# Four edits to a one-core graph network kernel: row sums by small SBUF-to-SBUF transfers, natural unit order, a new load order, and another root in the last tail

## The chip, the cores and the metric

The kernel runs on one core of one Trainium2 chip. The time is the device time in microseconds of one execution of the whole program; the number for a kernel is the median of its runs. TensorE (PE in the profile) multiplies matrices into PSUM, VectorE (DVE), ScalarE (ACT) and GpSimd (POOL) work elementwise, and SyncE (SP) issues the transfers (DMAs). Engines run on their own and wait for each other by semaphores.

## The reference

There are 64 graphs of 128 nodes with 128 features. Each passes four layers, with a layer norm over features behind each, added to its input (residual):

```
L0:  hi = x W1[:H], hj = x W1[H:]
     h[i,j] = relu(hi[i] + hj[j] + b1)           # 128 x 128 pairs, 128 features
     y[i,j] = h[i,j] W2 + b2 ;  y = layernorm(y, gamma, beta)
     out[i] = sum_j adj[i,j] y[i,j]
L1:  relu((D^-1/2 adj D^-1/2 x) W^T + b)
L2:  relu(((1+eps) x + adj^T x) W1 + b1) W2 + b2, masked
L3:  three times  h = relu(layernorm(adj^T (h W) + b + h))
```

L0 is nearly all of the work: 16,384 pairs a graph. The kernel folds the layer norm of a pair into one coefficient, c[i,j] = adj[i,j] / deviation[i,j]. Then out[i] is the sum over j of c[i,j] h[i,j], multiplied once by the centred W2 times gamma, plus the row sum of c times the centred b2 times gamma, plus adj times beta. Those **row sums of c** are what the first edit is about.

## The kernel before

**Units, duos, slots.** A unit is one node i with all 128 partners j: h of a unit is a 128x128 tile, made by one instruction relu(vT + uT[:, i]). Eight units are a duo, worked on in one of 16 slots of a graph. In each slot TensorE makes the duo's products (L417, two matmuls of 512 columns, each run as two passes, so two rows of the profile each), ScalarE squares them (L566), and in every second slot TensorE sums the squares over features (L429). Three engines share the h units: VectorE (`vector_units`: 4, 0 or 1), GpSimd (`pool_units`: 3 in the slots listed in ROOTLESS, otherwise 2) and ScalarE the rest. GpSimd makes fewer where it also has the two-step root of a norm (L912 adds eps, L915 raises to -0.5).

**Order of the work.** Everything is written out by hand, with no scheduler. Each engine runs the same loop over iterations and 16 slots; a slot is cut into nine fine places. Work of a graph lags: h in slot 4 on, products in slot 5 on, squares in slot 6, the weighted sums of h by c (L685, on VectorE) 19 slots later. The later layers of a graph ("the tail") run beside the pairs of two later graphs, at places given in the table `AT` as (slot, fine place), counted from two iterations after the graph began.

**The path of a coefficient.** ScalarE takes the root of half a graph's variances (L573). SyncE straightens the rows to one unit-half per partition (L324). VectorE takes the reciprocal (L693) and multiplies by adj (L701); the same instruction leaves the sum of each partition's 64 columns in `c_row_sum`. One partition holds half a unit's row, so a unit's row sum is the sum over two partitions. SyncE stores c to DRAM (L335) and broadcasts it to all partitions in five transfers (L347, L349). On the way SP waits in program order for each step.

**The row sums before.** At the end of slot 8 VectorE copies `c_row_sum` (L869). At place (1, 4) TensorE adds the pairs of partitions and puts them in unit order by two matmuls with a 0/1 matrix `row_pick` (L450), which the profile shows as four rows of 128x1. VectorE copies the result (L740) and uses it for `x_base` (L744). The matrix is needed because units are numbered in the order in which the transfers lay them out (`unit_of`); adj is loaded for this order in eight transfers a graph (L288).

**Start and end.** All seven first weights carry one semaphore, and TensorE waits for all of them and for VectorE's centring of W2 and b2 (L808 to L821). The last graph's tail runs with nothing beside it; its seven norms use GpSimd's root like all others.

Of the kernel before, what the change touches and what calls it, by code (L numbers as in the profile page):

```python
# [8 lines left out]
ALU = mybir.AluOpType  # L9
# [3 lines left out]
P = 128  # L13
# [90 lines left out]
def build(nc, x, adj, nodemask, l0_W1, l0_b1, l0_W2, l0_b2, l0_gamma, l0_beta, l1_W, l1_b,  # L104
# [4 lines left out]
    with ExitStack() as ctx:  # L109
# [6 lines left out]
        def sem(name):  # L116
# [42 lines left out]
        row_pick, rows_sum = sb("row_pick", [P, 2, P]), sb("rows_sum", [P, 2])  # L159
# [55 lines left out]
        row_pick_set, rows_kept, c_summed, c_sum_set = (  # L215
            sem("row_pick_set"), sem("rows_kept"), sem("c_summed"), sem("c_sum_set"))
# [60 lines left out]
        def _(sp):  # L277
# [6 lines left out]
            def load_adj_c_rows(a):  # L284
                rows = a.rearrange("(h q p n) (l j) -> h p q (n l) j", h=2, q=4, p=CHUNKS, l=2)
# [42 lines left out]
            def store_coefficients(g, half):  # L328

                wait_apart(sp, c_made, 2 * g + half + 1)  # L330
                for p in range(CHUNKS):
# [4 lines left out]
                             ).then_inc(c_stored[half], 16)  # L336

# [51 lines left out]
        def _(pe):  # L389
# [44 lines left out]
            def later_layers(g, b, lo, hi):  # L434
# [18 lines left out]
                if due("l0_mm"):  # L453
                    wait(pe, c_sum_set, g + 1)
# [32 lines left out]
            def later_set_up():  # L487
# [482 lines left out]
```

## Time and profile before

| | |
|---|---|
| median of 3 runs | 2756.13 us (2755.44 to 2756.31) |
| the profiled execution | 2755.1 us, its span 2753.5 us |
| PE busy | 2690.3 us, 98% |
| DVE busy | 2619.0 us, 95% |
| ACT busy | 2567.7 us, 93% |
| POOL busy | 2487.8 us, 90% |
| granted TensorE clock | 9 tenths or more in every slice but the last, 5 tenths there |
| DMA | 208 GB/s on average |
| one steady graph | 41.85 us, 62 times nearly alike |

A busy share counts any time in which an instruction is in flight. Matmuls overlap, so a busy TensorE is not TensorE at its peak. PEld is the weight load of a matmul; it can go while the matmul ahead of it runs. In a row of the timeline the bracket at the end gives how long the engine had been idle and what it waited for; "xN" means N like instructions merged, from the start of the first to the end of the last.

### The profile page before, as it was taken

What the parts mean: (1) busy time and instruction counts of PE and PEld (TensorE: products, weight loads), DVE (VectorE), ACT (ScalarE), POOL (GpSimd) and SP (SyncE); (2) the same over time, 40 slices, a digit from 0 to 9 for tenths busy, and PEclk for the clock granted to TensorE, in tenths of its full rate; (3) what the DMA queues carried; (4) which work ended last, traced back from release to release, by engine and by line L of the source; (5) the groups of instructions that cost most, each with busy time, mean ns of one, the idle gap of its engine ahead of it and who ended that gap; (6) DMA issues with size and microseconds to landing.
All of it is one profiled execution on the core that took longest, in us unless ns stands there. A gap on an engine that the chain in (4) does not pass through costs nothing.

```text
span 2753.5 us, 60836 instructions
## 1 busy us (share of the span) xinstructions
PE 2690.3 (98%) x10882; PEld 1147.3 (42%) x10882; DVE 2619.0 (95%) x20102; ACT 2567.7 (93%) x6903; POOL 2487.8 (90%) x3498
## 2 busy tenths in 40 slices
PE   8999999999999999999999999999999999999993
PEld 2344444444444444444444444444444444444442
DVE  4999999999999999999999999999999999999997
ACT  7999999999999999999999999999999999999991
POOL 3899999999999999999999999999999999999992
PEclk9999999999999999999999999999999999999995
DMA  3655655655555555556556555555655565565562
GB/s 108 237 196 209 231 206 196 231 219 194 215 231 201 202 226 219 197 215 231 199 200 232 214 194 221 227 199 203 230 213 197 214 236 196 202 234 210 195 228 95
DMA packets 188668, 571.72 MB, mean 208 GB/s; under 512 B 70656, under 2 KB 106368, under 8 KB 139136
## 3 DMA queue, kind: packets, MB, share of 16 engines
q1 hardware_dynamic: 188288, 567.83, 54.5%
q14 instruction: 285, 2.33, 0.3%
q8 instruction: 95, 1.56, 0.2%
HBM read 555.17 MB, written 8.39 MB: 205 GB/s over the span
## 4 chain that ended last, share of the span: by engine, by line
PE 67%; ACT 18%; DVE 8%; issue 6%; POOL 1%; DMA 0%; SPq 0%; ACTq 0%; DVEq 0%; POOLq 0%
PE y_ps L417 47%; PE ss_ps L429 13%; ACT h L556 11%; DVE h L685 5%; ACT sq L566 4%; ACT dev_rows L573 2%; PE prod_bank L479 1%; PE prod_bank L483 1%; PE prod_bank L450 1%; ACT hid L595 1%; PE prod_bank L456 1%; PE prod_bank L457 1%; PE uv_ps L402 1%; PE uv_ps L403 1%; POOL h L924 1%
## 5 line engine op out<-in xcount | busy, mean ns | idle before, releaser
L924 POOL TENSOR_SCALAR h<-vT,uT 128x128 f32<-128x128 f32 x2520 | 2056.7, 831 | 23.7 <-ACT vT L546 23.3
L417 PE MATMUL y_ps<-h,w2c 128*128 128x512 f32 x4096 | 2016.4, 609 | 11.4 <-DVE h L669 1.6
L685 DVE CUSTOM_DVE_ANT_0 h<-h,cb 128x128 f32<-128x128 f32 x8192 | 1983.9, 289 | 10.0 <-DVE gT_keep L749 0.5
L556 ACT ACTIVATE h<-uv_ps,uT 128x128 f32<-128x128 f32 x4848 | 1409.2, 433 | 0.0
L566 ACT ACTIVATE sq<-y_ps,b2c_col 128x1024 f32<-128x1024 f32 x1024 | 1182.5, 1155 | 112.3 <-PE y_ps L417 112.1
L417 PEld LDWEIGHTS y_ps<-h,w2c 128*128 128x128 f32 x4096 | 682.2, 190 | 903.6 <-issue 723.7
L685 DVE DVE_READ_ACCUMULATOR2_ANT gT<- 128x1 f32 x8192 | 636.8, 78 | 0.1
L429 PE MATMUL ss_ps<-sq,sel 128*32 128x512 f32 x4096 | 545.5, 605 | 0.9 <-ACT sq L566 0.9
L915 POOL TENSOR_TENSOR rs<-var_eps,minus_half 128x1 f32<-128x1 f32 x448 | 302.7, 676 | 35.1
L669 DVE TENSOR_SCALAR h<-vT,uT 128x128 f32<-128x128 f32 x757 | 200.9, 294 | 4.7 <-ACT mask_all L611 2.6
L912 POOL TENSOR_TENSOR var_eps<-mv,eps_col 128x1 f32<-128x1 f32 x448 | 96.1, 215 | 117.9 <-DVE mv L712 115.0
L429 PEld LDWEIGHTS ss_ps<-sq,sel 128*32 128x32 f32 x4096 | 80.6, 108 | 225.5 <-ACT sq L566 105.0
L709 DVE BATCH_NORM_STATS2 stats<-z 128x6 f32<-128x128 f32 x448 | 127.4, 284 | 0.3
L483 PEld LDWEIGHTS prod_bank<-l3w,aggT 128*128 128x128 f32 x384 | 73.6, 194 | 93.0 <-issue 58.6
L693 DVE RECIPROCAL invs<-devs 128x64 f32<-128x64 f32 x128 | 70.1, 548 | 38.6 <-DMA devs<-dev_rows 35.6
L718 DVE TENSOR_SCALAR x<-z,mv,rs 128x128 f32<-128x128 f32 x256 | 96.7, 378 | 6.2 <-POOL rs L915 4.8
L907 POOL TENSOR_TENSOR dis_raw<-degree_floor,minus_half 128x1 f32<-128x1 f32 x64 | 35.1, 548 | 65.3 <-DVE degree_floor L733 65.3
L599 ACT ACTIVATE aggT<-prod_bank 128x128 f32<-128x128 f32 x192 | 66.3, 345 | 25.3 <-PE prod_bank L479 21.7
L604 ACT ACTIVATE h<-z_aff 128x128 f32<-128x128 f32 x192 | 70.4, 367 | 17.5 <-DVE z_aff L792 17.5
L792 DVE SCALAR_TENSOR_TENSOR z_aff<-z_aff,rs,l3beta 128x128 f32<-128x128 f32 x192 | 81.9, 427 | 4.6 <-POOL rs L915 2.9
L573 ACT ACTIVATE dev_rows<-ss_ps 128x512 f32<-128x512 f32 x128 | 79.8, 624 | 1.2 <-PE ss_ps L429 1.2
L712 DVE BATCH_NORM_AGGREGATE mv<-stats 128x2 f32<-128x6 f32 x448 | 77.8, 174 | 2.6
(100 smaller groups left out, 1489.8 us busy)
## 6 DMA issues: line engine op xcount, KB each, us to landing
cb<-c_scratch SPq DMA_DIRECT2D x384, 1024.0 KB, 9.3
cb<-c_scratch SPq DMA_DIRECT2D x256, 512.0 KB, 4.8
adj_c<-in_adj_dram SPq DMA_DIRECT2D x512, 8.0 KB
devs<-dev_rows SPq DMA_DIRECT2D x512, 8.0 KB
x_in<-in_x_dram SPq DMA_DIRECT2D x64, 64.0 KB, 10.8
c_scratch<-c SPq DMA_DIRECT2D x128, 32.0 KB, 1.5
adj_in<-in_adj_dram SPq DMA_DIRECT2D x64, 64.0 KB, 4.4
x_res<-in_x_dram SPq DMA_DIRECT2D x64, 64.0 KB, 5.4
```

Source lines behind the costliest of these rows:

```text
L417: op = pe.matmul(y_ps[:, t % 2, c0:c0 + COLS], w2c[:], h[:, (SLOTS * g + t) % H_RING, c0:c0 + COLS], start=True, stop=True)
L429: mm = pe.matmul(ss_ps[32 * q:32 * q + 32, :], sel[:, ROWS - 1 - p:ROWS - 1 - p + 32], sq[:, (t + q // 2) % SQ_RING, c0:c0 + COLS], start= ...
L483: pe.matmul(out, aggT[:, b, :], l3w[:, i, :], start=True, stop=False)
L556: op = act.activation(h[:, (SLOTS * g + t) % H_RING, n * P:(n + 1) * P], v, ACT.Relu, bias=uT[:, b, i:i + 1])
L566: act.activation(sq[:, t % SQ_RING, :], y_ps[:, t % 2, :], ACT.Square, bias=b2c_col[:], scale=float(P) ** -0.5).then_inc(sq_done, 1)
L573: act.activation(dev_rows[:, half, :], ss_ps[:], ACT.Sqrt, bias=EPS).then_inc(dev_done, 1)
L669: op = dve.tensor_scalar(h[:, (SLOTS * g + t) % H_RING, n * P:(n + 1) * P], vT[:, b, :], uT[:, b, i:i + 1], 0.0, ALU.add, ALU.max)
L685: op = dve.tensor_tensor_reduce(h[:, (SLOTS * g + t) % H_RING, cols], h[:, (SLOTS * g + t) % H_RING, cols], cb[:, t // 2, c0:c0 + P], 1.0, ...
L709: dve.bn_stats(stats[:, b, :], z[:, b, :]).then_inc(stats_set[name], 1)
L718: dve.tensor_scalar(dst[:, b, :], z[:, b, :], mv[:, b, 0:1], rs[:, b:b + 1], ALU.subtract, ALU.mult).then_inc(normed[name], 1)
L915: pool.tensor_tensor(rs[:, b:b + 1], var_eps[:, b:b + 1], minus_half[:], ALU.pow).then_inc(rs_set[name], 1)
L924: op = pool.tensor_scalar(h[:, (SLOTS * g + t) % H_RING, n * P:(n + 1) * P], vT[:, b, :], uT[:, b, i:i + 1], 0.0, ALU.add, ALU.max)
```

## The change

1. **Row sums.** `row_pick`, the copy L869 and the two matmuls L450 go. SyncE instead copies the even and the odd partitions of `c_row_sum` side by side into `c_pair`, with two transfers of 64 partitions by one element for each half, issued right behind that half's broadcasts. VectorE adds the two columns at place (1, 8).
2. **Natural order.** `unit_of(t, n)` becomes 8t + n. adj's rows are loaded by two transfers a graph instead of eight.
3. **Load order.** W2 comes first under its own semaphore, then W1 and b1 under a second, then b2 and gamma. W2 is centred at once. The work on b2 moves to iteration 0, slot 5. TensorE's waits for the later set-up move from slot 2 to slot 4 of iteration 1.
4. **Norm ln0** of every graph moves from (4, 6) to (4, 8), its sum from (4, 5) to (4, 7), and so slot 4 instead of slot 5 is ROOTLESS.
5. **Last graph's roots.** ScalarE takes Sqrt(var + eps) and VectorE its reciprocal.

```diff
-ROOTLESS = (1, 2, 3, 5, 7, 9, 11, 14)
+ROOTLESS = (1, 2, 3, 4, 7, 9, 11, 14)

-    half, b = t // HALF, 2 * (t % HALF) + n // BLOCK_UNITS
-    return 64 * half + 16 * (b % 4) + 4 * (b // 4) + n % BLOCK_UNITS
+    return DUO_UNITS * t + n

-    ("c_sum_mm", 1, 4), ("c_sum", 1, 8), ("x_base", 2, 3),
-    ("g_keep", 3, 4), ("l0_mm", 4, 0), ("l0_sum", 4, 5), ("ln0", 4, 6), ("x1_scaled", 5, 6),
+    ("c_sum", 1, 8), ("x_base", 2, 3),
+    ("g_keep", 3, 4), ("l0_mm", 4, 0), ("l0_sum", 4, 7), ("ln0", 4, 8), ("x1_scaled", 5, 7),

# SyncE
-                    for p in range(CHUNKS):
-                        sp.dma_start(adj_c[32 * p:32 * p + 32, half, :], rows[half, p]).then_inc(adj_c_in, 16)
+                    sp.dma_start(adj_c[:, half, :], rows[half]).then_inc(adj_c_in, 16)
+            def pair_row_sums(g, b, half):
+                wait_apart(sp, c_made, 2 * g + half + 1)
+                wait_apart(sp, c_sum_set, g - 1)
+                wait_apart(sp, c_pair_in[half], 32 * g)
+                for l in range(2):
+                    sp.dma_start(c_pair[SPAN * half:SPAN * half + SPAN, b, l:l + 1], c_row_sum[l:P:2, half:half + 1]
+                                 ).then_inc(c_pair_in[half], 16)
                     spread_coefficients(old, 0)
+                    pair_row_sums(old, 1 - buf, 0)
...
                     spread_coefficients(old, 1)
+                    pair_row_sums(old, 1 - buf, 1)

# TensorE
-                if due("c_sum_mm"):
-                    wait(pe, rows_kept, g + 1)
                     wait(pe, adjT_set, g + 1)
-                    for half in range(2):
-                        op = pe.matmul(c_sum_ps[b], row_pick[:, half, :], rows_sum[:, half:half + 1],
-                                       start=(half == 0), stop=(half == 1))
-                    op.then_inc(c_summed, 1)
...
             turn_x(0, 0)
-            pe.wait_ge(weights_in, 16 * WEIGHTS)
-            pe.wait_ge(w2c_set, 1)
-            pe.wait_ge(affine_set, 2)
+            pe.wait_ge(w1_in, 16 * FIRST_WEIGHTS)

# ScalarE
+                for name in NORMS:
+                    if g == G - 1 and lo <= AT[name] + 2 < hi:
+                        wait(act, mv_set[name], g + 1)
+                        act.activation(var_eps[:, b:b + 1], mv[:, b, 1:2], ACT.Sqrt, bias=EPS).then_inc(eps_added[name], 1)

# VectorE
-                wait(dve, rows_kept, g)
+                wait(dve, c_pair_in[half], 32 * g)
...
+                if g == G - 1 and lo <= at + NORM_AT - 1 < hi:
+                    wait(dve, eps_added[name], g + 1)
+                    dve.reciprocal(rs[:, b:b + 1], var_eps[:, b:b + 1]).then_inc(rs_set[name], 1)
...
-                    wait(dve, c_summed, g + 1)
-                    dve.tensor_copy(c_sum[:, b:b + 1], c_sum_ps[b]).then_inc(c_sum_set, 1)
+                    for half in range(2):
+                        wait(dve, c_pair_in[half], 32 * (g + 1))
+                    dve.tensor_tensor(c_sum[:, b:b + 1], c_pair[:, b, 0:1], c_pair[:, b, 1:2], ALU.add).then_inc(c_sum_set, 1)
...
+                    if is_graph(new, 0) and s == START + 1:
+                        first_set_up()

# GpSimd
-                    if lo <= AT[name] + 1 < hi:
+                    if g < G - 1 and lo <= AT[name] + 1 < hi:
```

The line numbers of the changed kernel differ. TensorE in slots 1 and 2 of an iteration, before (L417 makes products, L445 turns adj, L450 are the row sums, L429 sums squares):

```order
L417 MATMUL y_ps<-h,w2c 128x512
L445 MATMUL prod_bank<-ident,adj_in 128x128
L417 MATMUL y_ps<-h,w2c 128x512 x3
L450 MATMUL prod_bank<-rows_sum,row_pick 128x1 x2
L429 MATMUL ss_ps<-sq,sel 32x512 x4
L417 MATMUL y_ps<-h,w2c 128x512 x3
```

and after (L433 products, L461 the turn, L445 the squares):

```order
L433 MATMUL y_ps<-h,w2c 128x512
L461 MATMUL prod_bank<-ident,adj_in 128x128
L433 MATMUL y_ps<-h,w2c 128x512 x3
L445 MATMUL ss_ps<-sq,sel 32x512 x4
L433 MATMUL y_ps<-h,w2c 128x512 x3
```

The row sums are gone, and nothing else moved on TensorE here.

ScalarE in slots 4 to 6, before (L566 squares, L556 h units, L599 and L588 copies of the tail, L573 the root of the variances):

```order
L566 ACTIVATE sq<-y_ps,b2c_col 128x1024
L556 ACTIVATE h<-uv_ps,uT 128x128 x6
L599 ACTIVATE aggT<-prod_bank 128x128
L566 ACTIVATE sq<-y_ps,b2c_col 128x1024
L556 ACTIVATE h<-uv_ps,uT 128x128 x4
L566 ACTIVATE sq<-y_ps,b2c_col 128x1024
L573 ACTIVATE dev_rows<-ss_ps 128x512
L556 ACTIVATE h<-uv_ps,uT 128x128 x6
```

and after (L580, L568, L617, L587 in their places):

```order
L580 ACTIVATE sq<-y_ps,b2c_col 128x1024
L568 ACTIVATE h<-uv_ps,uT 128x128 x5
L617 ACTIVATE aggT<-prod_bank 128x128
L580 ACTIVATE sq<-y_ps,b2c_col 128x1024
L568 ACTIVATE h<-uv_ps,uT 128x128 x5
L580 ACTIVATE sq<-y_ps,b2c_col 128x1024
L587 ACTIVATE dev_rows<-ss_ps 128x512
L568 ACTIVATE h<-uv_ps,uT 128x128 x6
```

One h unit moved from slot 4 to slot 5.

SyncE from the store of a graph's second half of coefficients on, before (L335 stores, L347 and L349 broadcast, L288 loads adj's rows, L358 and L359 load the tail's inputs):

```order
L335 DMA c_scratch<-c 128x64
L347 DMA cb<-c_scratch 128x1024
L349 DMA cb<-c_scratch 128x1024
L349 DMA cb<-c_scratch 128x2048 x3
L288 DMA adj_c<-in_adj_dram 32x1x64 x8
L358 DMA adj_in<-in_adj_dram 128x128
L359 DMA x_res<-in_x_dram 128x128
```

and after:

```order
L338 DMA c_scratch<-c 128x64
L359 DMA cb<-c_scratch 128x1024
L361 DMA cb<-c_scratch 128x1024
L361 DMA cb<-c_scratch 128x2048 x3
L347 DMA c_pair<-c_row_sum 64x1 x2
L287 DMA adj_c<-in_adj_dram 128x64 x2
L370 DMA adj_in<-in_adj_dram 128x128
L371 DMA x_res<-in_x_dram 128x128
```

The two pair transfers stand between the broadcasts and the loads; six transfers fewer load adj.

## Rows read from the trace of the kernel before

**Rows 1.** Busy time of one steady period: us, then PE, PEld, DVE, ACT, POOL, PEclk, DMA.

```profile
1165.30:1207.15 41.85, 41.74 (x170) 17.82 (x171) 40.62 (x314) 40.09 (x110) 39.28 (x56) 1.00 0.55 213
```

**Rows 2.** Chain of waits in that period: start us, us, what.

```profile
1172.02 0.34 PE prod_bank L450 x4
...
1194.76 1.93 PE y_ps L417 x4
...
1207.15 0.70 PE y_ps L417
```

**Rows 3.** Timeline of TensorE's matmuls in the next period: start us, us, what.

```profile
1211.13 2.74 PE L417 MATMUL y_ps<-h,w2c 128*128 128x512 f32 x6
1213.71 0.50 PE L450 MATMUL prod_bank<-rows_sum,row_pick 128*128 128x1 f32 x4
1214.14 1.07 PE L429 MATMUL ss_ps<-sq,sel 128*32 128x512 f32 x8
1215.14 2.84 PE L417 MATMUL y_ps<-h,w2c 128*128 128x512 f32 x6
1217.82 0.38 PE L402 MATMUL uv_ps<-xT,w1a 128*128 128x128 f32 x2
...
1227.02 1.88 PE L417 MATMUL y_ps<-h,w2c 128*128 128x512 f32 x4
```

**Rows 4.** Timeline of TensorE's weight loads, the two that waited for h.

```profile
1216.69 0.46 PEld L417 LDWEIGHTS y_ps<-h,w2c 128*128 128x128 f32 x2 [0.40 <-ACT h L556]
...
1227.65 0.42 PEld L417 LDWEIGHTS y_ps<-h,w2c 128*128 128x128 f32 x2 [0.44 <-ACT h L556]
```

**Rows 5.** Timeline of ScalarE in the same period.

```profile
1196.71 1.11 ACT L566 ACTIVATE sq<-y_ps,b2c_col 128x1024 f32<-128x1024 f32 x1 [0.53 <-PE y_ps L417]
...
1217.16 1.12 ACT L566 ACTIVATE sq<-y_ps,b2c_col 128x1024 f32<-128x1024 f32 x1 [0.27 <-PE y_ps L417]
...
1222.90 1.11 ACT L566 ACTIVATE sq<-y_ps,b2c_col 128x1024 f32<-128x1024 f32 x1 [0.58 <-PE y_ps L417]
1223.91 1.13 ACT L556 ACTIVATE h<-uv_ps,uT 128x128 f32<-128x128 f32 x4
1224.95 1.11 ACT L566 ACTIVATE sq<-y_ps,b2c_col 128x1024 f32<-128x1024 f32 x1
```

**Rows 6.** Timeline of SyncE behind the second half's broadcasts.

```profile
1194.26 5.36 SPq L288 DMA_DIRECT2D adj_c<-in_adj_dram  x8
```

**Rows 7.** Tile x_in: landing of its 64 loads, 63 of them issued behind broadcasts.

```profile
DMA to landing us min/median/max: 1.9/10.8/13.1
```

**Rows 8.** Timeline of VectorE, the copy of the row sums.

```profile
1172.69 0.15 DVE L740 COPY c_sum<-prod_bank 128x1 f32<-128x1 f32 x1
```

**Rows 9.** Timeline of the start: issue of w2, first table load, first real matmul.

```profile
2.58 0.43 SPq L297 DMA_DIRECT2D w<-in_L_gnn_W_dram  x1
...
3.30 1.28 ACT L537 ACT_TABLE_LOAD   x1 [3.30 <-PE prod_bank L395]
...
9.38 0.77 PE L402 MATMUL uv_ps<-xT,w1a 128*128 128x128 f32 x2 [6.17 <-DVE b2cg L821]
```

**Rows 10.** Tile b_col (b1 and b2 by columns): landing of the two loads.

```profile
DMA to landing us min/median/max: 2.1/2.8/3.4
```

**Rows 11.** Timeline of the last tail, norm ln2.

```profile
2733.63 0.18 DVE L712 BATCH_NORM_AGGREGATE mv<-stats 128x2 f32<-128x6 f32 x1
...
2734.15 0.55 POOL L915 TENSOR_TENSOR rs<-var_eps,minus_half 128x1 f32<-128x1 f32 x1
...
2734.74 0.35 DVE L718 TENSOR_SCALAR x<-z,mv,rs 128x128 f32<-128x128 f32 x1 [0.93 <-POOL rs L915]
```

**Rows 12.** Groups by line: xcount, busy us, mean ns of one, idle before.

```profile
L693 DVE RECIPROCAL invs<-devs 128x64 f32<-128x64 f32 x128 | 70.1, 548 | 38.6 <-DMA devs<-dev_rows 35.6
...
L573 ACT ACT_TABLE_LOAD x1 | 1.3, 1283 | 0.0
...
L611 ACT ACTIVATE mask_all<-prod_bank 128x64 f32<-128x64 f32 x1 | 0.2, 218 | 0.0
```

More of the change, by code:

```diff
@@ L25 @@
 SQ_RING = 4
-ROOTLESS = (1, 2, 3, 5, 7, 9, 11, 14)
+ROOTLESS = (1, 2, 3, 4, 7, 9, 11, 14)
 SPAN = P // 2
-WEIGHTS = 7
+FIRST_WEIGHTS = 3
+WEIGHTS = 3
 LATER_WEIGHTS = 8 + 4 * LAYERS
@@ L158, in build @@
         c_row_sum = sb("c_row_sum", [P, 2])
-        row_pick, rows_sum = sb("row_pick", [P, 2, P]), sb("rows_sum", [P, 2])
+        c_pair = sb("c_pair", [P, 2, 2])
         gT, gT_keep = sb("gT", [P, P]), sb("gT_keep", [P, 2, P])
@@ L185, in build @@
         xturn_ps = [prod_bank[b][:, 3, :] for b in range(2)]
-        c_sum_ps = [prod_bank[b][:, 2, 0:1] for b in range(2)]
+        w1_in, w2_in = sem("w1_in"), sem("w2_in")
         weights_in, later_weights_in, masks_in = sem("weights_in"), sem("later_weights_in"), sem("masks_in")
@@ L214, in build @@
             sem("degree_set"), sem("degree_floor_set"), sem("dis_raw_set"), sem("dis_set"))
-        row_pick_set, rows_kept, c_summed, c_sum_set = (
-            sem("row_pick_set"), sem("rows_kept"), sem("c_summed"), sem("c_sum_set"))
+        c_pair_in = [sem(f"c_pair_in{i}") for i in range(2)]
+        c_sum_set = sem("c_sum_set")
         x_base_set = sem("x_base_set")
@@ L284, in load_adj_c_rows @@
             def load_adj_c_rows(a):
-                rows = a.rearrange("(h q p n) (l j) -> h p q (n l) j", h=2, q=4, p=CHUNKS, l=2)
+                rows = a.rearrange("(h i) (l j) -> h (i l) j", h=2, l=2)
                 for half in range(2):
-                    for p in range(CHUNKS):
-                        sp.dma_start(adj_c[32 * p:32 * p + 32, half, :], rows[half, p]).then_inc(adj_c_in, 16)
+                    sp.dma_start(adj_c[:, half, :], rows[half]).then_inc(adj_c_in, 16)
             sp.dma_start(x_in[:], x[0]).then_inc(x_in_in, 16)
+            sp.dma_start(w2[:], l0_W2).then_inc(w2_in, 16)
+            first_weights = [(w1a[:], l0_W1[0:P, :]), (w1b[:], l0_W1[P:2 * P, :]), (b1_col[:], col(l0_b1))]
+            assert len(first_weights) == FIRST_WEIGHTS
+            for dst, src in first_weights:
+                sp.dma_start(dst, src).then_inc(w1_in, 16)
             weights = [
-                (w1a[:], l0_W1[0:P, :]), (w1b[:], l0_W1[P:2 * P, :]), (b1_col[:], col(l0_b1)),
-                (w2[:], l0_W2), (b2_row[:], row(l0_b2)), (b2_col[:], col(l0_b2)), (gamma0[:], row(l0_gamma)),
+                (b2_row[:], row(l0_b2)), (b2_col[:], col(l0_b2)), (gamma0[:], row(l0_gamma)),
             ]
@@ L407, in products @@
                 if block_of_duo == 0:
+                    if g == 0 and t == 0:
+                        pe.wait_ge(w2c_set, 1)
                     if vector_units(g, t) > 0:
@@ L445, in later_layers @@
                     pe.transpose(turn_ps[b], adj_in[:, b, :], ident[:]).then_inc(adj_turned, 1)
-                if due("c_sum_mm"):
-                    wait(pe, rows_kept, g + 1)
+                if due("l0_mm"):
                     wait(pe, adjT_set, g + 1)
-                    for half in range(2):
-                        op = pe.matmul(c_sum_ps[b], row_pick[:, half, :], rows_sum[:, half:half + 1],
-                                       start=(half == 0), stop=(half == 1))
-                    op.then_inc(c_summed, 1)
-                if due("l0_mm"):
-                    wait(pe, c_sum_set, g + 1)
                     wait(pe, g_kept, g + 1)
@@ L512, in iteration @@
                         later_set_up()
+                    if is_graph(new, 1) and s == LATER_SET_UP_SLOT + 2:
+                        later_set_up_done()
                     yg, t = lagging(graphs, s, START + 1)
@@ L562, in squares @@
             def squares(g, t):
+                if g == 0 and t == 0:
+                    act.wait_ge(b2c_set, 1)
                 wait(act, y_done, SLOTS * g + t + 1)
@@ L697, in coefficients @@
                 wait(dve, inv_done, 2 * g + half + 1)
-                wait(dve, adj_c_in, 128 * (g + 1))
+                wait(dve, adj_c_in, 32 * (g + 1))
                 wait(dve, c_stored[half], 16 * g)
-                wait(dve, rows_kept, g)
+                wait(dve, c_pair_in[half], 32 * g)
                 dve.tensor_tensor_reduce(c[:, half, :], adj_c[:, half, :], invs[:, half, :], 1.0, 0.0,
@@ L830, in later_set_up @@
                 dve.tensor_scalar(ident_eps[:], ident[:], l2eps[:], None, ALU.mult).then_inc(eps_set, 1)
-                by_unit = ident[:].rearrange("k (p q n l) -> k q p n l", p=CHUNKS, q=4, l=2)
-                dve.memset(row_pick[:], 0.0).then_inc(row_pick_set, 1)
-                dve.wait_ge(row_pick_set, 1)
-                for half in range(2):
-                    dve.tensor_tensor(
-                        row_pick[:, half, SPAN * half:SPAN * half + SPAN].rearrange("k (q p n) -> k q p n", q=4, p=CHUNKS),
-                        by_unit[:, :, :, :, 0], by_unit[:, :, :, :, 1], ALU.add).then_inc(row_pick_set, 1)
                 dve.wait_ge(mask_set, 1)
@@ L865, in iteration @@
                             later_layers(g, b, place + k, place + k + 1)
-                        if ct == HALF + 1 and cg is not None and k == FINE - 1:
-                            wait(dve, c_made, 2 * (cg + 1))
-                            wait(dve, c_summed, cg)
-                            dve.tensor_copy(rows_sum[:], c_row_sum[:]).then_inc(rows_kept, 1)
             program(dve, iteration)
```

32 lines of the change are left out of this document (17 added, 15 removed).

## The prediction

> **What bounds the kernel now.** I read the busy shares first, then one steady period by engine, then the chain of waits through it, and then TensorE against ScalarE instruction by instruction. In the steady part one graph takes 41.85 us, and in that stretch TensorE is busy 41.74 us of it at the full granted clock, VectorE 40.62, ScalarE 40.09 and GpSimd 39.28 [rows 1]. So TensorE is the busiest, but the other three have only 1.2 to 2.6 us to spare, and it matters where in the period that spare time lies. The chain of waits tells this: it runs through TensorE, with the row-sum matmuls L450 as 0.34 us of it, until a product ends at about 1196.7; then it runs through ScalarE for 10.4 us and comes back to TensorE at 1207.15 [rows 2]. ScalarE's own rows show the same from its side: it waits 0.53 us for TensorE at 1196.71, and then not again before 1217.16 [rows 5]. For those 20 us it works without a gap and TensorE follows it.
>
> The span is 2753.5 us and the profiled execution took 2755.1; the median of the three runs is 2756.13, 1.0 above. I work the sum against 2755.1 and add 1.0 at the end. Start, steady part and end are separate sums.
>
> **The row sums: what leaves TensorE.** Each graph drops one group of four L450 matmuls. They stand from 1213.71 to 1214.14 [rows 3]; the weight-and-start seam that the next group then needs leaves 0.34 us, which is what the chain counts [rows 2]. 62 graphs have theirs while TensorE still makes products of later graphs, so the whole would be 62 x 0.34 = 21.1 us. I don't take that, because the path that sets the period can go round L450. L450 stands at 1213.71, inside the 20 us in which ScalarE runs without a gap. The product at 1216.96 (the fifth of the six that start at 1215.14: 0.10 after the group's first, then 0.43 each, from 1211.13 to 1213.71 and 1215.14 to 1217.82 [rows 3]) needs an h that ScalarE finishes only then: its weight load, which could go at 1216.53, goes at 1216.69 [rows 4]. A product whose weights could not be fetched ahead costs the 0.10 seam, so that product can start at 1216.69 + 0.10 = 1216.79 at the earliest, 0.17 before its present start. ScalarE got there from 1196.71 without TensorE's help [rows 5], so nothing on TensorE moves it. Of the 0.34 us, **0.17 us** come through; the other 0.17 turn into a wait for h. ScalarE's wait at 1217.16 (0.27 us) shrinks too, and what follows on both engines moves up by 0.17.
>
> **The swap of GpSimd's h units.** The first norm of a graph moves two places later, so its root moves from slot 4 to slot 5, and GpSimd makes three h units in slot 4 and two in slot 5 instead of the reverse. ScalarE gives up one h unit in slot 4 and takes one in slot 5. In slot 4 that buys nothing, since ScalarE waits 0.58 us for TensorE right behind it, at 1222.90. In slot 5 the four units of 1223.91 become five: about 0.24 us more (four take 1.13 with a last one of 0.4, so one each 0.24 to 0.25). TensorE's own product ended so that ScalarE could not have gone on much sooner, about 0.05 before 1224.95 [rows 5]; so against its present time ScalarE is 0.24 - 0.05 later, less the 0.17 gained: 0.02 to 0.03. From here to the next wait ScalarE has no gap, and it feeds the product at 1227.88 (third of four from 1227.02 at 0.43 [rows 3]), whose weight load goes at 1227.65 [rows 4]. It would go at 1227.68 and the product start at 1227.78, while TensorE would be there at 1227.88 - 0.17 = 1227.71. That costs **0.07 us**. The period loses 0.17 - 0.07 = 0.10 us: 62 x 0.10 = **6.2 us**. Bounds: 0.34 a graph if h comes early enough (21.1), and nothing if the extra unit comes through in full (0).
>
> **The small transfers.** SyncE issues two for each half right behind the broadcasts. For the second half that is at 1194.26, where now 5.36 us of eight adj_c transfers begin [rows 6]; two pair transfers and two adj_c transfers replace those eight, so everything queued behind them on SP (the tail loads, then the next deviations) goes out sooner. The sums are wanted by VectorE at 1172.69 + 41.85 = 1214.54 [rows 8], 20 us after issue. The nearest row for a small load behind broadcasts is x_in: 10.8 us to landing, 13.1 at most [rows 7]. That leaves 6 us, and I cost it at 0; what covers it is the time until slot 1 of the next iteration. On VectorE the copy of L869 goes and an add of 128x1 takes the place of a copy of 128x1 (0.15 us [rows 8]): a little less work on an engine with 1.23 us to spare [rows 1]. The l0_sum that moves two places later only trades a wait for work.
> In the Trainium skill, "DMA: Bandwidth & Descriptors", section "Rules for kernel authors", says that many small transfers should be merged and that below 64 KB one pays mostly overhead; under "Specifications" it puts line rate at 512 B and more, and these move 4 bytes to a partition. [...] The four-byte b_col loads of this trace did land in 2.1 and 3.4 us [rows 10], so here the rule names a price that is hidden, not one that is absent; it is the last rival below.
>
> **The start.** TensorE's first real matmul waits until 9.38 because all seven weights and six VectorE steps on them come first [rows 9]. After the change it needs W1, b1 and xT. b1 takes the issue slot at 2.58 and lands 2.1 to 3.4 us later [rows 9, 10], so at 4.7 to 6.0; xT is ready when ScalarE's table load (3.30 + 1.28) and one 0.3 us copy are done, 4.9. TensorE starts at 5.0 to 6.0. I take 5.1, since the lower landing is that of a load between plain ones as here: **4.3 us** (3.3 to 4.4). The b2 steps come back as 1.2 us on VectorE behind the first h units, where TensorE still works through the first slot's products. TensorE's waits for the later set-up move down two slots, at no gain: VectorE keeps its own wait for the mask, and TensorE needs its h.
>
> **The end.** In the last graph's tail seven norms stand on the chain one after the other. From the end of mv (2733.81) through GpSimd's two steps to x at 2734.74 is 0.93 us [rows 11]. Now: 0.07 to ScalarE, a root of 128x1, 0.05, a reciprocal of 128x1, 0.04. ScalarE's smallest operation here is 0.22 us for 64 columns [rows 12], I take 0.20 for one. For the reciprocal the ends are 0.15 (any 128x1 on VectorE [rows 8]) and 0.55 (64 columns [rows 12]); per column that is 9 ns, so I take 0.15. The sum is 0.51, a gain of 0.42 x 7 = **2.9 us** (0.1 to 3.5).
> The Trainium skill, "ScalarE: Activation LUTs", section "What ACT_TABLE_LOAD costs", gives about 2.7 us for each change of table set, which would turn this part into a loss if roots and copies were in different sets. The trace has the load at 3.30 [rows 9] and a single one at the first root [rows 12], though every graph mixes roots with copies and squares, so I leave it out of the sum.
>
> **Sum.** 4.3 + 6.2 + 2.9 = 13.4 us. 2755.1 - 13.4 = 2741.7, and 1.0 for the median: **2742.7 us**.
>
> **Rivals.**
> - *The whole 0.34 comes through.* For it: TensorE is busy 41.74 of 41.85 us, and the wait at 1216.69 is one of a few tenths only. Against: rows 4 and 5 as above. 4.3 + 21.1 + 2.9 = 28.3: 2727.8 us.
> - *ScalarE takes it all back.* The extra unit in slot 5 meets no slack, and the period stays at 41.85. For it: the h wait at 1227.65 already is the longest of those behind slot 5. Only start and end remain, 7.2 us: 2748.9 us.
> - *The pair transfers land late, slower than before.* VectorE stands at c_sum until they do, and all its work behind it shifts. It decides once landing takes more than 20 us from issue. At 22 us VectorE loses 2 us a graph, of which its 1.2 us to spare cover part: 62 x 0.8 - 7.2 = +42 us, 2798 us. For it: four-byte pieces queued behind all of a half's broadcasts; the rule of the Trainium skill named above. Against: x_in's 13.1 us at most.
>
> **Chances.** Forecast (a gain of 0.05 to 0.17 a graph, 2738 to 2747 us) 58%; whole gain 20%; all taken back 17%; late landing 4%; anything else 1%. The range of 2729 to 2750 reaches into both neighbours and leaves out the late landing. A measurement here tells about 0.2%, 5.5 us, from no change: faster than 2750.6 are the first two cases and most of the third, 0.90; same 0.06; slower 0.04.
>
> **What would show it.** A steady period of 41.75 us (41.51 by the first rival, 41.85 by the second); a new weight-load wait for h in slot 3 of about half the 0.34 us, and TensorE idle at the third product behind slot 5; no VectorE wait for c_pair; first uv matmul at 5.1; in the last 33 us seven gaps before x and z_aff of about half a microsecond. I am wrong if VectorE shows a wait at c_sum, or if the period is outside 41.68 to 41.80.

## The result

| | median | runs, range | ratio to before, 95% interval |
|---|---|---|---|
| before | 2755.89 us | 4, 2755.44 to 2756.31 | |
| after | 2773.76 us | 4, 2773.28 to 2776.01 | 1.0066, 1.0049 to 1.0084 |

The change costs 17.9 us. I had predicted a gain of 13.4, so the forecast and its range were wrong, and not one of my rivals tells the reason: the one on the slow side (late pair transfers) put its cost in the wrong place. The title names four edits; the fifth, number 4 in the list of the change (norm ln0), is the one that costs the time.

The profiled execution of after took 2776.01 us, 2.3 above the median, and its span is 2774.2 us. So the pieces below differ by 20.7 us in sum, where the medians differ by 17.9.

**Where the time went, in three pieces.** Every graph has one `c_sum` on VectorE. Its first and last start, read from the row of its line, cut the span into start, 63 periods and end. Before and after (the second fence):

```profile
L740 DVE COPY c_sum<-prod_bank x64: 144/148/152, 85.2 to 2717.5; 128x1 f32<-128x1 f32 x64
```

```profile
L762 DVE TENSOR_TENSOR c_sum<-c_pair x64: 146/148/152, 80.6 to 2741.3; 128x1 f32<-128x1 f32 x64
```

| | start | 63 periods | one | end | span |
|---|---|---|---|---|---|
| before | 85.2 | 2632.3 | 41.78 | 36.0 | 2753.5 |
| after | 80.6 | 2660.7 | 42.23 | 32.9 | 2774.2 |
| difference | -4.6 | +28.4 | +0.45 | -3.1 | +20.7 |

Start and end gained what I had forecast (4.3 and 2.9). The steady part, where I had forecast 0.10 us a graph less, takes 0.45 more. (The 41.85 us of [rows 1] is one steady period. The mean over 63 is lower because the first takes 41.1 us and the last 37.8; after, 41.1 and 37.4. Without these two it is 41.86 before and 42.33 after.)

**The chain of waits** now has other engines in it. From the profile's pages, shares of the span by engine, before and after:

```profile
PE 67%; ACT 18%; DVE 8%; issue 6%; POOL 1%; DMA 0%; SPq 0%; ACTq 0%; DVEq 0%; POOLq 0%
```

```profile
DVE 63%; POOL 29%; issue 5%; PE 2%; ACT 1%; DMA 0%; SPq 0%; DVEq 0%; POOLq 0%; ACTq 0%
```

Before, the chain was TensorE's and ScalarE's. Now TensorE has 2% of it, although the profile's page still shows it busy for 98% of the span: that share did not tell who sets the period.

**The waits** (engine, line waited for: us in total, times, longest) show what is new:

```profile
PEld y_ps L433 <- DVE h L686: 209.3, 249, 1.4
...
DVE x L739 <- POOL rs L931: 82.3, 64, 1.3
```

VectorE waits once in each graph, 1.3 us, for GpSimd's root of the first norm, and TensorE's weight loads now wait for h units of VectorE (the first row), which comes later with it. Before, VectorE's largest wait was for TensorE's l0 product (the first row below); for the root it waited 4.8 us in 5 times, all of them in the last tail, behind 2723 us.

```profile
DVE z L753 <- PE prod_bank L457: 42.5, 63, 1.4
...
DVE x L718 <- POOL rs L915: 4.8, 5, 1.0
```

**GpSimd's timeline** of one period, first before, then after. The bracket is the idle time before the row and what ended it.

```profile
1169.97 0.55 POOL L907 TENSOR_TENSOR dis_raw<-degree_floor,minus_half 128x1 f32<-128x1 f32 x1 [0.92 <-DVE degree_floor L733]
1170.50 10.04 POOL L924 TENSOR_SCALAR h<-vT,uT 128x128 f32<-128x128 f32 x12
1181.05 0.19 POOL L912 TENSOR_TENSOR var_eps<-mv,eps_col 128x1 f32<-128x1 f32 x1 [0.51 <-DVE mv L712]
1181.32 0.69 POOL L915 TENSOR_TENSOR rs<-var_eps,minus_half 128x1 f32<-128x1 f32 x1
1182.00 3.14 POOL L924 TENSOR_SCALAR h<-vT,uT 128x128 f32<-128x128 f32 x4
```

```profile
1177.93 0.55 POOL L923 TENSOR_TENSOR dis_raw<-degree_floor,minus_half 128x1 f32<-128x1 f32 x1 [0.72 <-DVE degree_floor L754]
1178.46 12.00 POOL L940 TENSOR_SCALAR h<-vT,uT 128x128 f32<-128x128 f32 x14
1190.43 0.19 POOL L928 TENSOR_TENSOR var_eps<-mv,eps_col 128x1 f32<-128x1 f32 x1
1190.69 0.56 POOL L931 TENSOR_TENSOR rs<-var_eps,minus_half 128x1 f32<-128x1 f32 x1
...
1220.30 0.55 POOL L923 TENSOR_TENSOR dis_raw<-degree_floor,minus_half 128x1 f32<-128x1 f32 x1 [0.72 <-DVE degree_floor L754]
```

And VectorE's row that waits for that root:

```profile
1191.29 0.39 DVE L739 TENSOR_SCALAR x<-z,mv,rs 128x128 f32<-128x128 f32 x1 [1.32 <-POOL rs L931]
```

This is a loop over two queues. VectorE makes degree_floor; GpSimd, which waited for it, makes the degree root, then all h units that stand in its queue before the root of ln0, then that root; VectorE, which waits for it, works without a gap up to the next degree_floor. Before, 12 units stood between the two roots and GpSimd waited 0.51 us at the end of them: the loop was open there. Now 14 stand there, GpSimd waits no more, VectorE does. The windows of after, first VectorE's part of the loop, then GpSimd's (start:end, length, busy time of PE, PEld, DVE, ACT, POOL with counts, PE clock, DMA share, GB/s):

```profile
1191.29:1220.29 29.00, 28.69 (x114) 11.89 (x111) 28.77 (x218) 28.08 (x80) 26.25 (x38) 1.00 0.45 160
1177.93:1191.29 13.36, 13.36 (x57) 5.08 (x55) 11.89 (x95) 12.05 (x31) 13.28 (x18) 1.00 0.83 320
```

These are 29.00 us in which VectorE is busy for 28.77, and 13.36 in which GpSimd is busy for 13.28: together 42.36 us, the period.

**Start and end.** TensorE's first real matmul begins at 4.67 and not at 9.38 [rows 9], and ScalarE's table load has moved to before it has input:

```profile
4.67 0.80 PE L416 MATMUL uv_ps<-xT,w1a 128*128 128x128 f32 x2 [1.59 <-DMA b_col<-in_L_gnn_b_dram]
```

```profile
0.72 1.28 ACT L549 ACT_TABLE_LOAD   x1 [0.72 <-PEq L975]
```

The last norm of the tail, the counterpart of [rows 11]:

```profile
2771.19 0.18 DVE L729 BATCH_NORM_AGGREGATE mv<-stats 128x2 f32<-128x6 f32 x1
2771.41 0.20 ACT L598 ACTIVATE var_eps<-mv 128x1 f32<-128x1 f32 x1 [0.90 <-DVE mv L729]
2771.64 0.17 DVE L732 RECIPROCAL rs<-var_eps 128x1 f32<-128x1 f32 x1 [0.27 <-ACT var_eps L598]
2771.92 0.35 DVE L739 TENSOR_SCALAR x<-z,mv,rs 128x128 f32<-128x128 f32 x1
```

From the end of mv (2771.37) to x it is 0.55 us, where it was 0.93.

**The pair transfers** (the tile's row): no engine waited for them.

```profile
DMA to landing us min/median/max: 9.5/10.3/12.4
```

### The profile page after: what moved, and what is told of

It is laid out like the page before. It is cut to its first block, busy times and chain, and to the rows that moved or that the text cites. A ratio compares the mean times of both kernels' runs of the same rounds, so it can differ in the third digit from the quotient of the medians.

```text
span 2774.2 us, 60254 instructions
## 1 busy us (share of the span) xinstructions
PE 2705.7 (98%) x10626; PEld 1092.2 (39%) x10626; DVE 2620.9 (94%) x20042; ACT 2569.3 (93%) x6910; POOL 2496.3 (90%) x3484
## 4 chain that ended last, share of the span: by engine, by line
DVE 63%; POOL 29%; issue 5%; PE 2%; ACT 1%; DMA 0%; SPq 0%; DVEq 0%; POOLq 0%; ACTq 0%
DVE h L702 39%; POOL h L940 26%; DVE stats L726 3%; DVE x L739 3%; DVE gT L702 3%; DVE z_aff L814 2%; DVE z_aff L809 2%; DVE h L686 2%; DVE mv L729 2%; DVE invs L710 2%; DVE z L801 1%; POOL rs L931 1%; POOL dis_raw L923 1%; DVE c L718 1%; PE y_ps L433 1%
## 5 line engine op out<-in xcount | busy, mean ns | idle before, releaser
L940 POOL TENSOR_SCALAR h<-vT,uT 128x128 f32<-128x128 f32 x2520 | 2078.9, 841 | 22.5 <-ACT vT L558 22.3
L433 PE MATMUL y_ps<-h,w2c 128*128 128x512 f32 x4096 | 2037.1, 613 | 12.8 <-DVE h L686 3.3
L568 ACT ACTIVATE h<-uv_ps,uT 128x128 f32<-128x128 f32 x4848 | 1431.2, 453 | 0.0
L580 ACT ACTIVATE sq<-y_ps,b2c_col 128x1024 f32<-128x1024 f32 x1024 | 1200.0, 1172 | 119.6 <-PE y_ps L433 119.3
L433 PEld LDWEIGHTS y_ps<-h,w2c 128*128 128x128 f32 x4096 | 671.3, 189 | 934.2 <-issue 500.7
L445 PE MATMUL ss_ps<-sq,sel 128*32 128x512 f32 x4096 | 545.5, 605 | 0.9 <-ACT sq L580 0.9
L931 POOL TENSOR_TENSOR rs<-var_eps,minus_half 128x1 f32<-128x1 f32 x441 | 289.9, 657 | 34.5
L445 PEld LDWEIGHTS ss_ps<-sq,sel 128*32 128x32 f32 x4096 | 80.6, 108 | 272.4 <-ACT sq L580 158.9
L739 DVE TENSOR_SCALAR x<-z,mv,rs 128x128 f32<-128x128 f32 x256 | 100.0, 391 | 85.6 <-POOL rs L931 82.3
L617 ACT ACTIVATE aggT<-prod_bank 128x128 f32<-128x128 f32 x192 | 69.9, 364 | 37.5 <-PE prod_bank L488 37.5
L587 ACT ACTIVATE dev_rows<-ss_ps 128x512 f32<-128x512 f32 x128 | 82.5, 645 | 1.2 <-PE ss_ps L445 1.2
## 6 DMA issues: line engine op xcount, KB each, us to landing
c_pair<-c_row_sum SPq DMA_DIRECT2D x256, 0.2 KB, 10.3
```

The lines of the kernel that those rows point to most:

```text
L433: op = pe.matmul(y_ps[:, t % 2, c0:c0 + COLS], w2c[:], h[:, (SLOTS * g + t) % H_RING, c0:c0 + COLS], start=True, stop=True)
L445: mm = pe.matmul(ss_ps[32 * q:32 * q + 32, :], sel[:, ROWS - 1 - p:ROWS - 1 - p + 32], sq[:, (t + q // 2) % SQ_RING, c0:c0 + COLS], start= ...
L568: op = act.activation(h[:, (SLOTS * g + t) % H_RING, n * P:(n + 1) * P], v, ACT.Relu, bias=uT[:, b, i:i + 1])
L580: act.activation(sq[:, t % SQ_RING, :], y_ps[:, t % 2, :], ACT.Square, bias=b2c_col[:], scale=float(P) ** -0.5).then_inc(sq_done, 1)
L739: dve.tensor_scalar(dst[:, b, :], z[:, b, :], mv[:, b, 0:1], rs[:, b:b + 1], ALU.subtract, ALU.mult).then_inc(normed[name], 1)
L931: pool.tensor_tensor(rs[:, b:b + 1], var_eps[:, b:b + 1], minus_half[:], ALU.pow).then_inc(rs_set[name], 1)
```

## The experiments

The kernel before was timed again beside each group of experiments, at 2755.3 to 2756.4 us, and every ratio is to that time.

Theory: GpSimd works in order, and edit 4 puts two more h units in front of the root for which VectorE waits; that closes a loop of 42.36 us. Rivals: the pair transfers cost time on SyncE or in landing; ScalarE's extra unit in slot 5 costs far more than 0.07 us; the later place itself costs VectorE time.

### Undo edit 4

```diff
-ROOTLESS = (1, 2, 3, 4, 7, 9, 11, 14)
+ROOTLESS = (1, 2, 3, 5, 7, 9, 11, 14)
-    ... ("l0_sum", 4, 7), ("ln0", 4, 8), ("x1_scaled", 5, 7),
+    ... ("l0_sum", 4, 5), ("ln0", 4, 6), ("x1_scaled", 5, 6),
```

> The changed kernel with edit 4 undone (l0_sum, ln0, x1_scaled and ROOTLESS as in the kernel before). Theory GpSimd: in the changed kernel GpSimd makes 14 h units in one piece between the degree root and the root of ln0, 12 before; VectorE waits 1.3 us a graph for that root and closes a loop with the next degree root, of 42.36 us. With 12 units the loop has 1.7 us less, TensorE sets the period again: 41.68 us if only 0.17 of the 0.34 us of row-sum matmuls comes through, as I had predicted, 41.51 if all of it does. Then 2755.9 - 4.8 (start, measured) - 2.9 (end) - 62 x 0.17 or 0.34 = 2738 or 2727 us. Rival, transfers: the small transfers or the load order slow SyncE's chain or the DMA engines, so that the period stays at 42.3 us and the time near 2772.

Measured 2739.22 us, ratio to before 0.9936 (0.9923 to 0.9948): faster than before and 34.5 us faster than after. So edit 4 is the loss. GpSimd's queue is as before, with 12 units and a wait of its own:

```profile
1203.13 0.55 POOL L923 TENSOR_TENSOR dis_raw<-degree_floor,minus_half 128x1 f32<-128x1 f32 x1 [0.92 <-DVE degree_floor L754]
1203.67 10.03 POOL L940 TENSOR_SCALAR h<-vT,uT 128x128 f32<-128x128 f32 x12
1214.08 0.19 POOL L928 TENSOR_TENSOR var_eps<-mv,eps_col 128x1 f32<-128x1 f32 x1 [0.39 <-DVE mv L729]
```

This is the version that beats both kernels. Its three pieces are 81.3, 2621.2 (41.61 a graph) and 33.2 us; against before that is 3.9, 11.1 and 2.8 us less.

### Edit 4 alone, on the kernel before

```diff
-ROOTLESS = (1, 2, 3, 5, 7, 9, 11, 14)
+ROOTLESS = (1, 2, 3, 4, 7, 9, 11, 14)
-    ... ("l0_sum", 4, 5), ("ln0", 4, 6), ("x1_scaled", 5, 6),
+    ... ("l0_sum", 4, 7), ("ln0", 4, 8), ("x1_scaled", 5, 7),
```

> The kernel before with edit 4 alone. Theory GpSimd: 14 units in one piece, a loop of 42.36 us as in the changed kernel, VectorE waiting about 1.3 us a graph for the root of ln0: 2755.9 + 62 x 0.51 = about 2787 us. Rival, transfers: no change, 2756 us. Rival, ScalarE's extra unit in slot 5 (what I had priced at 0.07 us a graph): 2760 us, with no VectorE wait for a root.

Measured 2784.62 us, ratio 1.0100 (1.0086 to 1.0114). That is 28.2 us more than the 2756.41 beside it. With neither pair transfers nor natural order the wait is the same, and the rival of the transfers falls:

```profile
DVE x L718 <- POOL rs L915: 82.8, 67, 1.3
```

The 63 periods take 2658.0 us, 42.19 each, nearly what after needs (42.23) although the L450 matmuls are back: once the loop sets the period, these 0.34 us of TensorE cost next to nothing.

### Only the list of slots without a root put back

```diff
-ROOTLESS = (1, 2, 3, 4, 7, 9, 11, 14)
+ROOTLESS = (1, 2, 3, 5, 7, 9, 11, 14)
```

> The changed kernel with ROOTLESS alone as before; ln0 stays at (4, 8). GpSimd's units before the root are still 14, since slots 4 and 5 hold five together either way. Theory GpSimd by the place of the root: no gain, 2772 to 2776 us, period 42.3. Rival, the swap of units between slots 4 and 5 (ScalarE's extra unit in slot 5) is what costs: 2740 us.

Measured 2775.35 us, ratio 1.0068 (1.0054 to 1.0081), the same as after (1.0066). Slots 4 and 5 hold five units together either way, and all are in front of the root. The rival of ScalarE's unit falls.

### The norm one place earlier

```diff
-ROOTLESS = (1, 2, 3, 4, 7, 9, 11, 14)
+ROOTLESS = (1, 2, 3, 5, 7, 9, 11, 14)
-    ... ("l0_sum", 4, 7), ("ln0", 4, 8), ...
+    ... ("l0_sum", 4, 6), ("ln0", 4, 7), ...
```

> The changed kernel with ROOTLESS as before and ln0 at (4, 7), l0_sum at (4, 6): the root is then at (4, 8), still in slot 4, and has 12 units ahead of it. Theory GpSimd: as fast as with the places of before, 2727 to 2738 us, although the norm is later than before; VectorE waits less for TensorE at l0_sum. Rival, that any later norm lengthens the tail's path: between 2740 and 2775 us.

Measured 2739.44 us, ratio 0.9937 (0.9923 to 0.9950). The root's step stands at the norm's place plus one: from (4, 8) that is the first step of slot 5, behind the units which GpSimd makes at the start of a slot; from (4, 7) it is the last step of slot 4, in front of them. Against the run before it, which has the same list of slots, one place of nine decides 35.9 us. The time is 1.4 us above what I had expected, but the mechanism is as expected: no VectorE wait for the root in any steady graph, and less of a wait for TensorE's l0 product (17.9 us in all, 29.2 with edit 4 undone). The rival that any later norm costs time falls: with edit 4 undone it was 2739.22.

### Thirteen units, in two ways

The place (4, 7) with slot 4 kept as the one without a root:

```diff
-    ... ("l0_sum", 4, 7), ("ln0", 4, 8), ...
+    ... ("l0_sum", 4, 6), ("ln0", 4, 7), ...
```

> The kernel after with l0_sum at (4, 6) and ln0 at (4, 7), and slot 4 still the one without a root: GpSimd has 13 h units between the degree root and the root of ln0 (14 after, 12 before). Theory (the order of GpSimd's queue closes a loop of 42.36 us with 14 units, and one unit is 12.00 / 14 = 0.86 us): the loop would take 41.50 us, under the 41.65 us in which the version with 12 units repeats, so the whole penalty is gone: about 2739 to 2741 us. The extra ScalarE unit of slot 5, which I priced at 0.07 us a graph, would show here as up to 4 us against the 2739.2 of the version with 12 units. Rival (each unit in front of the root costs its 0.86 us, or a share of it, with no threshold): halfway between 12 and 14 units, about 2757 us.

And all places as in after, but one GpSimd unit less in slot 2:

```diff
-ROOTLESS = (1, 2, 3, 4, 7, 9, 11, 14)
+ROOTLESS = (1, 3, 4, 7, 9, 11, 14)
```

> The kernel after with every place as it is (root of ln0 in slot 5), but GpSimd makes two h units in slot 2 instead of three and ScalarE one more: 13 units in front of the root. Theory (it is the time of GpSimd's units in the loop, not the place of the norm on VectorE): loop 41.50 us, the penalty is gone but for what ScalarE's extra unit costs (at most 0.25 us a graph, 15 us): 2739 to 2755 us. Rival (the later place itself costs VectorE and TensorE the time): it stays at about 2774 us.

Measured 2743.73 us, ratio 0.9959 (0.9946 to 0.9971), and 2742.84 us, ratio 0.9955 (0.9943 to 0.9968). With the norm's place unchanged, one unit less gives back 31 us, so it is GpSimd's time in the loop and not the place on VectorE. The first misses its expectation (2739 to 2741) by 2.7 us: the threshold is not sharp. In both, VectorE still waits 0.4 to 0.5 us a graph for the root. In the version with one unit less, GpSimd's part of the loop is 12.66 us and VectorE's 29.12, of which 0.3 is a wait for the deviations. Together that is 41.78 us, where I had expected 41.50: with 13 units the loop is still as long as the period.

```profile
DVE x L739 <- POOL rs L931: 31.6, 63, 1.0
```

(This row is of the version with one unit less.) Their medians are 4.5 and 3.6 us over the version with 12 units, and by the ratios it is 5 to 6 us; in the first, that holds the swap of ScalarE's unit (0.07 us in the prediction) and what is left of the wait, which the run does not separate.

### Fifteen units

```diff
-ROOTLESS = (1, 2, 3, 4, 7, 9, 11, 14)
+ROOTLESS = (1, 2, 3, 4, 5, 7, 9, 11, 14)
```

> The kernel after with slot 5 added to the slots without a root: 15 h units of GpSimd between the degree root and the root of ln0, ScalarE one unit less. Theory (GpSimd's queue closes the loop): the period grows by one unit, 0.86 us, 63 times: 54 us, about 2828 us, though ScalarE and TensorE have less to do. Rival (the loop runs elsewhere, GpSimd's wait is a follower): ScalarE's unit less makes it the same or faster, 2760 to 2774 us.

Measured 2815.72 us, ratio 1.0218 (1.0204 to 1.0232): 42 us more than after, in the direction of the theory and against the rival, though 12 us less than expected. The period is (2781.0 - 80.9) / 63 = 42.86, 0.63 more. I had priced the unit at 0.86; here the fifteenth added 0.68. GpSimd's part of the loop grew by just that, from 13.36 to 14.04 us, and VectorE's stayed (29.00 and 28.92):

```profile
1194.92 12.68 POOL L940 TENSOR_SCALAR h<-vT,uT 128x128 f32<-128x128 f32 x15
```

```profile
DVE x L739 <- POOL rs L931: 124.8, 64, 2.0
```

### Row sums and natural order alone, on the kernel before

```diff
-    return 64 * half + 16 * (b % 4) + 4 * (b // 4) + n % BLOCK_UNITS
+    return DUO_UNITS * t + n
...
+            def pair_row_sums(g, b, half):
+                ...
-                if due("c_sum_mm"):
-                    ...
-                    dve.tensor_copy(c_sum[:, b:b + 1], c_sum_ps[b])
+                    dve.tensor_tensor(c_sum[:, b:b + 1], c_pair[:, b, 0:1], c_pair[:, b, 1:2], ALU.add)
-                    for p in range(CHUNKS):
-                        sp.dma_start(adj_c[32 * p:32 * p + 32, half, :], rows[half, p])
+                    sp.dma_start(adj_c[:, half, :], rows[half])
```

> The kernel before with edits 1 and 2 alone (row sums by pair transfers, natural order). My step (0.17 of the 0.34 us a graph come through, 62 times, the transfers cost nothing): 10.5 us, 2745.4 us. Rival, the whole 0.34: 2734.8 us. Rival, the transfers cost something: above 2750 us.

Measured 2744.91 us, ratio 0.9964 (0.9952 to 0.9977), against 2755.32 for the kernel before: 10.4 us, where the step said 10.5. The way round L450 is in its trace. TensorE's weight loads and matmuls in slot 3:

```profile
1214.34 0.30 PEld L425 LDWEIGHTS y_ps<-h,w2c 128*128 128x128 f32 x2 [0.76 <-ACT h L556]
```

```profile
1211.43 1.06 PE L437 MATMUL ss_ps<-sq,sel 128*32 128x512 f32 x8
1212.43 3.04 PE L425 MATMUL y_ps<-h,w2c 128*128 128x512 f32 x6
1215.30 0.38 PE L410 MATMUL uv_ps<-xT,w1a 128*128 128x128 f32 x2
```

(L425 is the line of the products here, L437 that of the squares, L410 that of the next graph's first matmul.) The L450 matmuls no longer stand in front of L437, and the group of six products behind it has grown from 2.84 us [rows 3] to 3.04. From the group's start to the next L410 it was 2.68 us (1215.14 to 1217.82), now it is 2.87. So 0.19 us of the 0.34 came back at the product whose h was not ready.

### Start and end alone, on the kernel before

```diff
+            sp.dma_start(w2[:], l0_W2).then_inc(w2_in, 16)
...
-            pe.wait_ge(weights_in, 16 * WEIGHTS)
+            pe.wait_ge(w1_in, 16 * FIRST_WEIGHTS)
...
+                        act.activation(var_eps[:, b:b + 1], mv[:, b, 1:2], ACT.Sqrt, bias=EPS)
+                    dve.reciprocal(rs[:, b:b + 1], var_eps[:, b:b + 1])
```

> The kernel before with edits 3 and 5 alone (load order, and ScalarE's and VectorE's roots for the last graph). The prediction's terms: 4.3 + 2.9 = 7.2 us, 2748.7 us. The traces so far show 3.9 at the start and 2.8 at the end together with the other edits, which gives 2749.2 us. Rival: the start's gain is taken back by the first slots without the rest, less than 4 us in all.

Measured 2748.26 us, ratio 0.9974 (0.9964 to 0.9984), against 2755.32: 7.1 us less, where the two terms said 7.2. By its trace the start took 3.6 us less and the end 2.7.

### Every pair transfer four times, on the faster version

```diff
-                for l in range(2):
-                    sp.dma_start(c_pair[SPAN * half:SPAN * half + SPAN, b, l:l + 1], ...)
+                for copy in range(4):
+                    for l in range(2):
+                        sp.dma_start(c_pair[SPAN * half:SPAN * half + SPAN, b, l, copy:copy + 1], ...)
```

> The faster version with every pair transfer made four times, into four places of c_pair, the last of them used: sixteen small transfers a graph instead of four. Prediction's step (hidden, 6 us to spare): SyncE issues 12 more at 0.6 us, 7 us a graph, of which half stand between the broadcasts and adj_c; no change, 2739 to 2741 us. Rival (their issue or their landing is near the path): VectorE waits at c_sum or for the deviations, above 2745 us.

Measured 2738.02 us, ratio 0.9936 (0.9924 to 0.9949), the ratio of the faster version itself. SyncE spends 5.1 us behind each half's broadcasts where it spent 1.2, and no loss follows from it:

```profile
1185.86 5.06 SPq L348 DMA_DIRECT2D c_pair<-c_row_sum  x8
1191.01 1.02 SPq L287 DMA_DIRECT2D adj_c<-in_adj_dram  x2
```

### Can ScalarE be relieved?

The chain of the faster version runs through TensorE, and for 10.4 us of a period through ScalarE. Slot 13 lies in that stretch. One GpSimd unit more there, and then the same with one less in slot 5:

```diff
-ROOTLESS = (1, 2, 3, 5, 7, 9, 11, 14)
+ROOTLESS = (1, 2, 3, 5, 7, 9, 11, 13, 14)
```

> The faster version (the kernel after, with the places and the list of slots without a root as before), and slot 13 added to that list: GpSimd makes one h unit more a graph and ScalarE one less, in the stretch in which the chain of that version runs through ScalarE for 10.4 us (1188.0 to 1198.4). Theory A (ScalarE's 10.4 us set the period there, a unit is 0.24 to 0.25 us): 0.24 x 62 = 15 us off 2739.2, down to 2724. Theory B (GpSimd's queue is 0.9 us from closing its loop, and a unit is 0.86 us of it): nothing or worse, 2739 to 2750 us.

```diff
-ROOTLESS = (1, 2, 3, 5, 7, 9, 11, 14)
+ROOTLESS = (1, 2, 3, 7, 9, 11, 13, 14)
```

> The same, but slot 5 leaves the list as slot 13 enters it, so GpSimd makes as many units as before and ScalarE gets one more in slot 5, which cost about 0.07 us a graph in the prediction. Theory A: 0.24 - 0.07 to 0.10 = 0.14 to 0.17 a graph, 9 to 11 us off 2739.2: 2729 us. Theory B (what ScalarE gives up in slot 13 was not on the path, or GpSimd is late for slot 13): 2739 to 2746 us.

Measured 2740.02 us, ratio 0.9945 (0.9932 to 0.9959), and 2742.49 us, ratio 0.9952 (0.9940 to 0.9965). Nothing is gained; theory A fell. In the first, the chain has gone over to GpSimd, by line:

```profile
by line: POOL h L940 42.1%; DVE h L702 18.6%; PE y_ps L433 7.1%; POOL rs L931 6.4%; issue 3.6%; POOL var_eps L928 2.3%; PE ss_ps L445 1.9%; DVE invs L710 1.5%; DVE stats L726 1.4%; DVE z_aff L814 1.4%; DVE z_aff L809 1.3%; DVE gT L702 1.3%;
```

GpSimd's wait of 0.39 us in front of the root of ln0 is gone, and VectorE waits for that root again, though only 12 units stand in front of it:

```profile
DVE x L739 <- POOL rs L931: 36.0, 63, 1.0
```

In the second it is 35.5 us in 62 times. Both kernels repeat in 41.7 us. This fits theory B, that GpSimd has no room for the unit of slot 13, but no run separates it. What keeps the second, with its unchanged number of units, from gaining was not tried.

## Why the prediction was wrong

**The step that failed** is the one sentence on edit 4 that I did not cost: "The l0_sum that moves two places later only trades a wait for work." It looks at VectorE alone. The root that follows l0_sum is GpSimd's, it moved as well, and it moved past GpSimd's two units at the start of slot 5. I counted the swap of units by slot (3 and 2 instead of 2 and 3) and what ScalarE pays for it, but not on which side of the root they stand. What the sentence says of VectorE came true: its wait for TensorE's l0 product went from 42.5 us to 1.4. In its place came the wait of 82.3 us for the root, which the prediction has at nothing.

The rows of before would have given the price; I worked it out only after the result:

- GpSimd's part: 0.55 for the degree root, 10.04 for twelve units, two more at 10.04 / 12 = 0.84 each, and 0.95 from var_eps to the end of rs (1181.05 to 1182.00). Together 13.2 us.
- VectorE's part: from x at 1182.18 to the degree root of the next graph at 1169.97 + 41.85 = 1211.82 it was 29.64 us. x stands two weighted sums later, each 0.21 us apart, so 0.43 less: 29.2. VectorE waited 0.2 us in it for the deviations, which could go: 29.0. After the change it was 29.00.
- The loop: 42.2 to 42.4 us, against a period of 41.85. It closes, and the period grows by 0.35 to 0.55; measured, the mean grew by 0.45. Over the 62 periods with full overlap that is 22 to 34 us of loss against 7.2 of gain at start and end.

What hid it from me was the busy shares of the profile's page and the chain. GpSimd had 1% of the chain and 2.6 us a period to spare [rows 1], and I took that as room. But its spare time lay in front of particular instructions: 0.51 us at the root of ln0. Two units are 1.7 us. The engine's total was not short; the stretch between two waits was. And my lower bound for the steady part was "nothing gained": I gave "slower" 4% in all, and "anything else" than my four cases 1%.

**By the prediction's own steps:**

- *0.17 of 0.34 us for the row sums*: right, in the mechanism too (the product that waits for h takes back 0.19). 10.4 us alone, 11.1 in the 63 periods of the faster version; the rival of the whole 0.34 (21.1 us) fell.
- *The swap, 0.07 us a graph*: not visible in after. By the 63 periods it is 2660.7 - 2657.2 = 3.5 us, 0.06 a graph, in the pair with 14 units, but the medians of this pair lie 1.6 us the other way. In both kernels the loop sets the period and not ScalarE, so the pair can't price the mechanism of the prediction. Not settled, and small either way.
- *Small transfers at no cost*: right. They landed in 9.5 to 12.4 us, near x_in's 10.8 to 13.1 [rows 7], and no engine waited for them; fourfold they cost nothing either. "DMA: Bandwidth & Descriptors" of the Trainium skill, section "Rules for kernel authors", warns against many small transfers; each did cost SyncE 0.6 us to issue, on a queue that had the time.
- *Start 4.3 us*: right in size, 3.6 alone and 4.6 in after. One term of it was wrong: I had TensorE wait for xT until 4.9, behind ScalarE's table load at 3.30. That load now runs at 0.72, xT is ready at 3.40, and what TensorE waits for is b1, which landed 2.09 us after its issue at 2.58. I had not foreseen that the load would move.
- *End 2.9 us*: right, 2.7 to 3.1. The root on ScalarE took 0.20 us and the reciprocal 0.15 to 0.17, the values taken; the trace of after has two table loads in all (1.28 us each, before the first copy and at the first root L587), none in the tail.
- *The rival on the slow side* was another one. With edit 4 left out its 0.07 us a graph goes too, so the prediction's other terms give 2755.1 - 4.3 - 10.5 - 2.9 + 1.0 = 2738.4 us, and 2739.22 was measured.

## What to carry to other kernels

When an instruction moves in program order, list for each engine in the handshake what it has moved past, and add up the loop from one cross-engine wait to the next around both queues; compare that sum with the period, not the engine's busy share. An engine with 6% idle and 1% of the chain can close such a loop with one more unit of work. And cost every edit in the list, above all the one that looks like a correction of place.

## What was not expected of the hardware

- One and the same GpSimd instruction (h, 128x128) takes 705 to 1024 ns. Twelve of them took 10.04 us, thirteen 11.19, fourteen 12.00 and fifteen 12.68, so the price of one more depends on which one it is: 0.68 to 1.15 us. What makes the difference was not tried.
- A product whose weights could not be loaded ahead took the 0.34 us saved in front of it down to about 0.15.
- Transfers of four bytes to each of 64 partitions, issued behind a 1 MB broadcast, landed at 8.7 us in the median with sixteen of them a graph and at 10.3 with four: the number of them did not set the landing.
